# Edge pass: eight graphs a turn instead of four, the expert layer in two halves

## What is computed

```python
h = (x_flat @ W_gat).reshape(M, HEADS, NUM_EXPERTS)            # 4 heads, 4 experts
e = leaky_relu(a_src[src] + a_dst[dst])                         # one row per edge and head
ee = exp(e - segment_max(e, dst)[dst]); denom = segment_sum(ee, dst)
agg = segment_sum(h[src] * ee / denom[dst], dst) + b_gat
scores = layernorm(agg, gamma, beta).mean over the heads        # then top 2 of 4, softmax
for ei in range(4):
    out += g[ei] * (gelu(x @ W1[ei] + b1[ei]) @ W2[ei] + b2[ei])
```

## Time and profile before

| | us |
|---|---|
| median of 3 runs | 3323.31 (3321.15 to 3329.72) |
| profiled execution, span | 3908.9 |
| of it up to the first gather of edge rows | 1927.15 |
| busy over the span: PE, DVE, ACT, POOL | 1964.9, 2118.6, 1188.0, 1852.3 |

### The profile page before, as it was taken

One profiled execution on the slowest core, in us unless ns is written; L12 is line 12 of the kernel. 1 busy time (PEld: TensorE's weight loads), 2 busy tenths in 40 slices (PEclk: granted clock), 3 DMA queues, 4 the chain that ended last, 5 costly groups with the idle time before them and its releaser, 6 DMA issues. The chain is left out here.

```text
span 3908.9 us, 31732 instructions
## 1 busy us (share of the span) xinstructions
PE 1964.9 (50%) x9058; PEld 1350.2 (35%) x9113; DVE 2118.6 (54%) x4420; ACT 1188.0 (30%) x2437; POOL 1852.3 (47%) x1785
## 2 busy tenths in 40 slices
PE   0777742377777426676232445345244433444446
PEld 0666641255454215666211122122122212222223
DVE  7799887997789984444312334333233323433336
ACT  0676753244344204554201212112121111221212
POOL 5000247354444214445675555654655665556552
PEclk9988855699898657776556666666666666766668
DMA  6970001011111021001111111111111111111111
GB/s 212 345 292 1 17 26 34 22 35 47 34 44 30 31 84 38 17 21 22 41 28 32 28 31 37 26 34 27 32 30 31 37 26 34 27 38 33 28 31 38
DMA packets 172773, 197.65 MB, mean 51 GB/s; under 512 B 60217, under 2 KB 127072, under 8 KB 172032
## 3 DMA queue, kind: packets, MB, share of 16 engines
q1 hardware_dynamic: 107184, 118.69, 9.1%
q0 software_dynamic: 60160, 67.73, 8.4%
q10 hardware_dynamic: 5328, 9.97, 0.7%
HBM read 96.94 MB, written 105.25 MB: 52 GB/s over the span
## 5 line engine op out<-in xcount | busy, mean ns | idle before, releaser
L1453 POOL DMA_INDIRECT edge_rows<-node_table,edge_ids x1024 | 990.2, 967 | 687.3 <-POOLq L1193 385.9
L1581 PE MATMUL x_b_hid<-x_featT,x_w 128*128 128x512 f32 x512 | 353.6, 837 | 599.8 <-PEq L1193 395.7
L1096 POOL DMA_INDIRECT token_results<-arena,token_of x160 | 247.2, 1545 | 370.3 <-ACT arena L1030 271.4
L1581 PEld LDWEIGHTS x_b_hid<-x_featT,x_w 128*128 128x128 f32 x512 | 113.1, 254 | 830.7 <-issue 635.6
L1109 POOL DMA_INDIRECT adjacent<-keys,row_ids x256 | 243.0, 949 | 315.5 <-DVE counts L785 168.1
L1588 PE MATMUL x_b_res<-x_w,x_hid 128*128 128x128 f32 x2048 | 311.2, 304 | 146.1 <-issue 146.1
L1089 POOL DMA_INDIRECT slots<-arena,send x128 | 169.7, 1325 | 433.5 <-ACT arena L987 398.7
L1588 PEld LDWEIGHTS x_b_res<-x_w,x_hid 128*128 128x128 f32 x2048 | 275.9, 212 | 245.6 <-issue 245.4
L1415 DVE SCALAR_TENSOR_TENSOR x_weighed<-x_b_res,gates,x 128x128 f32<-128x128 f32 x128 | 36.1, 344 | 523.5 <-DVEq L1193 493.0
L562 DVE TENSOR_TENSOR sort_ping<-sort_pong 128x1024 f32<-128x1024 f32 (+1 forms) x184 | 285.8, 1594 | 47.5 <-ACT sort_pong L973 43.5
L562 DVE TENSOR_TENSOR sort_pong<-sort_ping 128x1024 f32<-128x1024 f32 (+1 forms) x184 | 285.7, 1594 | 37.0 <-ACT sort_ping L973 33.3
(11 more groups left out here) (333 smaller groups left out, 4303.3 us busy)
## 6 DMA issues: line engine op xcount, KB each, us to landing
edge_table<-zeros SPq DMA_DIRECT2D x8, 5120.0 KB
edge_rows<-node_table,edge_ids POOLq DMA_INDIRECT x1024
arena<-slots SPq DMA_DIRECT2D x40, 260.0 KB
slots<-zeros SPq DMA_DIRECT2D x2, 5120.0 KB
edge_table<-edge_rows SPq DMA_DIRECT2D x64, 160.0 KB
out_dram<-x_y ACTq DMA_DIRECT2D x33, 256.0 KB
adjacent<-in_adj_dram SPq DMA_DIRECT2D x32, 256.0 KB, 2.8
arena<-token_results SPq DMA_DIRECT2D x32, 256.0 KB
```

The lines of the kernel that those rows point to most:

```text
L1096: pool.indirect_dma_start(rows_dram, bass.IndirectOffsetOnAxis(token_of[:, n % 4, r:r + 1], 0), res[:, n % 2, r, :], None, bounds_check=TO ...
L1453: pool.indirect_dma_start(rows[:, u, c, :], None, table_dram, bass.IndirectOffsetOnAxis(ids[:, u, c:c + 1], 0)).then_inc(rows_in[u], 16)
L1581: pe.matmul(b_hid[:, c % 2, :], w1[:, c // HC1, c % HC1 * P:(c % HC1 + 1) * P], featT[:, :], start=True, stop=True).then_inc(hid_mm, 1)
```

## The change

A unit becomes eight graphs and a part 32 gathers, so there are 16 units, 16 turns and 32 parts. DVE and ACT treat the windows, the attention and the gates of eight graphs at once. The expert layer keeps tiles for four graphs (PER), and each of its engines handles a unit in two halves: ACT and PE one half after the other, each with its normalised x, transposes, hidden and output products; DVE, once all gates of the unit are made, waits for the first half's products, sums them, gives res_free, waits for the second half's, and sums them. One store of 512 KB a turn replaces two of 256. In PE the last expert's bias product moves behind its output products, and PE itself gives hid_free before it; DVE gave it before. The early scratch tiles wide, self_w and clamp_w move into win_msg.

```diff
-PART_TILES = 16
+PART_TILES = 32
-UNIT = 4
+UNIT = 8
+HALVES = UNIT // PER
@@ edges_and_experts1
-    SPAN = UNIT * NODES
+    SPAN = PER * NODES
-        self_w, clamp_w, wide = sb("self_w", [P, GRAPHS, HEADS]), sb("clamp_w", [P, GRAPHS, HEADS]), sb("wide", [P, GRAPHS, GAT])
+        early = msg[:, :, :, :].rearrange("p t k c -> p (t k c)")
+        wide = early[:, 0:GRAPHS * GAT].rearrange("p (n c) -> p n c", c=GAT)
...
-        feat, featT = sb("x1_feat", [P, UNIT, FEAT]), sb("x1_featT", [P, SPAN])
-        hid, weighed, y = sb("x1_hid", [P, E * HC1, SPAN]), sb("x1_weighed", [P, UNIT, FEAT]), sb("x1_y", [P, UNIT, FEAT])
+        feat, featT = sb("x1_feat", [P, PER, FEAT]), sb("x1_featT", [P, SPAN])
+        hid, weighed, y = sb("x1_hid", [P, E * HC1, SPAN]), sb("x1_weighed", [P, PER, FEAT]), sb("x1_y", [P, UNIT, FEAT])
@@ DVE
-                take(dve, res_mm, 1)
-                dve.sem_inc(hid_free, 1)
-
-                settle()
-                for e in range(E):
-                    if e == E - 1:
-                        take(dve, out_done, 16)
-                    for v in range(UNIT):
...
+                for h in range(HALVES):
+                    take(dve, res_mm, 1)
                     settle()
-                dve.sem_inc(summed, 1)
-                dve.sem_inc(res_free, 1)
+                    for e in range(E):
+                        if e == E - 1 and h == 0:
+                            take(dve, out_done, 16)
+                        for v in range(PER):
+                            at = h * PER + v
...
+                            last = dve.scalar_tensor_tensor(to, b_res[:, e, v, :], one[:, at, e:e + 1], so_far, ALU.mult, ALU.add)
+                            step(last)
+                        settle()
+                    dve.sem_inc(summed, 1)
+                    dve.sem_inc(res_free, 1)
@@ ACT
             def send(unit):
-                take(act, summed, 1)
+                take(act, summed, HALVES)
...
+                for h in range(HALVES):
+                    for v in range(PER):
+                        b = mine * UNIT + (h * PER + v)
...
+                    take(act, hid_free, 1)
+                    for c in range(E * HC1):
+                        act.wait_ge(hid_mm, c + 1)
+                        act.activation(hid[:, c, :], b_hid[:, c % 2, :], ACT.Gelu, bias=b1[:, c:c + 1]).then_inc(hid_s, 1)
+                    act.sem_inc(hid_mm, -E * HC1)
                 send(before)
@@ PE
-                    pe.matmul(b_res[:, e, :, :], ones[0:1, :], b2[0:1, e, :].unsqueeze(1).to_broadcast([1, UNIT, FEAT]), start=True, stop=False)
-                    for v in range(UNIT):
+                    final = e == E - 1
+                    if not final:
+                        pe.matmul(b_res[:, e, :, :], ones[0:1, :], b2[0:1, e, :].unsqueeze(1).to_broadcast([1, PER, FEAT]), start=True, stop=False)
+                    for v in range(PER):
...
-                last.then_inc(res_mm, 1)
+                last.then_inc(hid_free, 1)
+                pe.matmul(b_res[:, E - 1, :, :], ones[0:1, :], b2[0:1, E - 1, :].unsqueeze(1).to_broadcast([1, PER, FEAT]),
+                          start=False, stop=True).then_inc(res_mm, 1)
+
+            def turn():
+                for _ in range(HALVES):
+                    half()
```

More of the change, by code:

```diff
@@ L1147, in edges_and_experts1 @@
         msg, got, sums, adv = sb("win_msg", [P, UNIT, WINDOW, GAT]), sb("win_got", [P, UNIT, GAT]), sb("win_sums", [P, UNIT, HEADS]), sb("win_adv", [P, UNIT])
+        early = msg[:, :, :, :].rearrange("p t k c -> p (t k c)")
+        wide = early[:, 0:GRAPHS * GAT].rearrange("p (n c) -> p n c", c=GAT)
+        self_w, clamp_w = (early[:, lo:lo + GRAPHS * HEADS].rearrange("p (n h) -> p n h", h=HEADS)
+                           for lo in (GRAPHS * GAT, GRAPHS * (GAT + HEADS)))
         gat_b, gamma, beta = sb("gat_b", [P, GAT]), sb("gat_gamma", [P, GAT]), sb("gat_beta", [P, GAT])
@@ L1208, in _ @@
             dve.memset(left[:, GRAPHS:GRAPHS + UNIT], 0.0).then_inc(prepared, 1)
-            dve.memset(y[:, :, :], 0.0).then_inc(summed, 1)
+            dve.memset(y[:, :, :], 0.0).then_inc(summed, HALVES)
             made[0] += 1
@@ L1403, in turn @@
                 step(dve.tensor_tensor(one[:, :, :], one[:, :, :], per4(first[:, :]), ALU.mult))
-                take(dve, res_mm, 1)
-                dve.sem_inc(hid_free, 1)
-                settle()
-                for e in range(E):
-                    if e == E - 1:
-                        take(dve, out_done, 16)
-                    for v in range(UNIT):
[L1413 to L1416, removed]
-                    settle()
-                dve.sem_inc(summed, 1)
-                dve.sem_inc(res_free, 1)
+                for h in range(HALVES):
+                    take(dve, res_mm, 1)
+                    settle()
+                    for e in range(E):
[3 more added lines that the diff above has]
+                            at = h * PER + v
+                            so_far = x[:, bass.ds(unit * UNIT + at, 1), :].rearrange("p o f -> p (o f)") if e == 0 else weighed[:, v, :]
+                            to = y[:, at, :] if e == E - 1 else weighed[:, v, :]
+                            last = dve.scalar_tensor_tensor(to, b_res[:, e, v, :], one[:, at, e:e + 1], so_far, ALU.mult, ALU.add)
[3 more added lines that the diff above has]
+                    dve.sem_inc(res_free, 1)
                 take(dve, step_s, done[0])
@@ L1520, in send @@
             def send(unit):
-                take(act, summed, 1)
+                take(act, summed, HALVES)
                 act.dma_start(out[:, bass.ds(unit * UNIT, UNIT), :], y[:, :, :]).then_inc(out_done, 16)
             def turn(mine, before):
-                for v in range(UNIT):
[L1526 to L1536, removed]
+                for h in range(HALVES):
+                    for v in range(PER):
+                        b = mine * UNIT + (h * PER + v)
+                        last = act.activation(feat[:, v, :], x[:, bass.ds(b, 1), :].rearrange("p o f -> p (o f)"), ACT.Identity,
+                                              bias=shift[:, bass.ds(b, 1)], scale=rstd[:, bass.ds(b, 1)])
+                    last.then_inc(normed, 1)
+                    take(act, turned, 1)
+                    act.activation(featT[:, :], b_featT[:, :, :].rearrange("p v i -> p (v i)"), ACT.Copy).then_inc(featT_s, 1)
+                    take(act, hid_free, 1)
[3 more added lines that the diff above has]
+                    act.sem_inc(hid_mm, -E * HC1)
                 send(before)
@@ L1570, in _, with half @@
             pe.wait_ge(weights_in, 64)
-            def turn():
+            def half():
                 take(pe, normed, 1)
-                for v in range(UNIT):
+                for v in range(PER):
                     last = pe.transpose(b_featT[:, v, :], feat[:, v, :], ident)
@@ L1584, in turn @@
                 for e in range(E):
-                    pe.matmul(b_res[:, e, :, :], ones[0:1, :], b2[0:1, e, :].unsqueeze(1).to_broadcast([1, UNIT, FEAT]), start=True, stop=False)
-                    for v in range(UNIT):
+                    final = e == E - 1
+                    if not final:
+                        pe.matmul(b_res[:, e, :, :], ones[0:1, :], b2[0:1, e, :].unsqueeze(1).to_broadcast([1, PER, FEAT]), start=True, stop=False)
+                    for v in range(PER):
                         for c in range(HC1):
-                            last = pe.matmul(b_res[:, e, v, :], hid[:, e * HC1 + c, v * P:(v + 1) * P], w2[:, e * HC1 + c, :], start=False,
-                                             stop=(v == UNIT - 1 and c == HC1 - 1))
-                last.then_inc(res_mm, 1)
+                            last = pe.matmul(b_res[:, e, v, :], hid[:, e * HC1 + c, v * P:(v + 1) * P], w2[:, e * HC1 + c, :],
+                                             start=final and v == 0 and c == 0, stop=not final and v == PER - 1 and c == HC1 - 1)
+                last.then_inc(hid_free, 1)
[4 more added lines that the diff above has]
+                    half()
             pe.wait_ge(planned, 1)
```

2 lines of the change are left out of this document (1 added, 1 removed).

## The result

The changed kernel takes 3421.06 us (median of 4, 3414.72 to 3422.92) against 3322.82 us for the kernel before in the same runs: ratio 1.0296, 95% interval 1.0284 to 1.0309. That is 98 us slower, in the forecast's direction and inside the range of 3344 to 3440, though 1 us above the 3370 to 3420 that the forecast case itself allowed. The forecast was +70.

What follows compares the result with a forecast made beforehand. POOL's issue was taken to bound the loop. The end's 144.3 us, less 64.1 before and 10.1 for earlier last-but-one windows, gave +70.1 on 3323.3: 3394 us, range 3344 to 3440.

Steps and rivals of the forecast that it cites:

- the forecast case: Whole pass: 3394 us, 70.1 us slower, allowed from 3370 to 3420; chance 0.65.
- What bounds the loop: In the loop of the kernel before, POOL's issue sets the turn without stalls: 45.6 us against 29.
- The cover: In the changed loop, POOL's turn of 91.2 us hides the wait between the halves, whose chain has a 76.6 us cycle.
- Rival A: In the loop, the halves' chain overtakes POOL: 96 us a cycle, 3466 us in all; chance 0.15.
- The end: From the last-but-one windows' issue to the span's end, PE's pieces stand uncovered in series: 144.3 us, 64.1 before.
- a sign: In the changed kernel's trace, the last message product comes some 33 us after the last turn's first operation.
- The loop's 25 us: From first to last-but-one windows, the loop was forecast to change by -91.2 us; measured -66.6.
- the small gain on DVE's share of POOL's lengthened issues: In the loop, DVE's lengthening of POOL's issues was taken to change by nothing, between -10 and +10 us in all.

Runs made afterwards that it cites:

- the undisturbed trace: The kernel before, run again with no edit for a trace without the first one's stalls: 3322.99 us, trace span 3321.2 us.
- the changed kernel with the short product: The changed kernel with a message product of one graph instead of eight, the other seven graphs' messages left out: 3379.4 us, ratio 1.0193.

## Why the prediction was right, and where its size was off

**What bounds the loop.** Right. Taking 492 us of waits out of the trace, because the median had no room for them, gave a turn of 45.6, an end of 64.1 and a first stage of 1806 us; the undisturbed trace has 45.83, 64.0 and 1797.7.

**The cover.** Right. The wait between the halves, 15.0 to 20.9 us of DVE's time a turn, didn't move the turn when it was taken away (93.61 against 93.45). Rival A, the chain through two halves overtaking POOL, didn't come about: DVE waits 34.5 to 40.5 us for its windows in the turns after the first (40.10 in the line at 3284.47).

**The end.** The steps stood, with sizes off in both directions. From a turn's start to its gates it took 29.0 us (29.1 forecast), from the message product to the gates 19.8 (19.9). The last message product stands 88.9 us after the last-but-one turn's start (85.8): two terms of that stretch were mis-sized against each other. The output products of the second half took 20.85 us of waiting instead of 12.7, because I had priced them from a stretch in which PE had been at work just before. Here PE had been idle for 48 us, and the granted clock of the two stretches on either side of the sums is:

```profile
3318.00:3339.00 21.00, 20.31 (x74) 14.51 (x75) 0.23 (x1) 0.00 (x0) 0.00 (x0) 0.57 0.00 0
3339.00:3361.00 22.00, 20.25 (x94) 11.45 (x93) 10.91 (x29) 8.91 (x14) 0.00 (x0) 1.00 0.00 0
3337.70 1.12 PE L1599 MATMUL x_b_res<-x_b,ones 1*128 1x512 f32 x2
3348.85 1.09 PE L1593 MATMUL x_b_res<-x_b,ones 1*128 1x512 f32 x2 [0.87 <-PEq L1198]
3359.71 1.12 PE L1599 MATMUL x_b_res<-x_b,ones 1*128 1x512 f32 x2
```

In the first PE was granted 0.57 of full speed in the mean, near the lower of its two levels (1.2 GHz of 2.4), in the second 1.00, and the same output and bias products take 3337.70 + 1.12 - 3318.69 = 20.1 us there and 3359.71 + 1.12 - 3348.85 = 12.0 here. The pieces behind, at full clock, were shorter than mine: 10.1 instead of 12.4 us from the transposes to the first output product. The wait between the last halves was 15.46 us instead of 12.7, and the store after the last sum 3.2 instead of 4. The sum missed by 4.8 us. The trace's 20.85 us is the longest value of a wait that takes 15.0 us in other turns, so most of the 4.8 us can be chance. By the longer wait and the shorter pieces the last message product begins 28.4 us after the last turn's first operation, where the prediction named 33 as a sign.

**The loop's 25 us.** This is the step that failed: "the small gain on DVE's share of POOL's lengthened issues (45.6 against 36 x 1.25 = 45.0) I take at nothing, between -10 and +10 us in all, since as many elements pass." The lengthening doesn't go by elements. A gather that begins while the product runs waits for its end, so a product of 1.76 us costs 0.4 us in most turns and 1.2 in some, and one of 3.36 us costs 2.34 in every turn: 14 x 2.34 = 33 us against 30 x 0.54 = 16. The gather that is hit begins 0.89 or 0.90 us after the product's start in all 14 turns. That fits the order of the two engines, since the landing of POOL's windows starts DVE's turn. The trace that I predicted from had such a gather beside the product of its middle turn, and I averaged it away:

```profile
2728.20 1.36 POOL L1453 DMA_INDIRECT edge_rows<-node_table,edge_ids  x1 [0.30 <-issue]
```

The bound should have been from nothing to the product's full length, 15 x 3.4 = 50 us; the 25 us lie outside the 10 that I allowed. The number stayed in the range only because the range went half way to rival A, which didn't come about.

The Trainium skill, page "SBUF — State Buffer", section "Who interferes with whom", says that a DVE instruction with two SBUF inputs contends with a GpSimd instruction that reads SBUF, because its second input comes through the shared read interface, and that a tensor_reduce never contends on this chip. The trace agrees with both: the products (two inputs) lengthen gathers, and the gathers that begin in the 5.27 us reductions of the changed kernel stay at 0.94 to 0.95 us. The same section adds that in an earlier probe a tensor_tensor did not stall the DMA. For these indirect DMAs the measurement decides otherwise (2.34 us a turn, gone with the product). That it is the read of the indices that waits would fit both, but no run here separates it.

Of the Trainium skill's two rules on grouping (page "Perfetto Trace Analysis", section "Optimizing Scalar/DVE Operations") the second held. Grouping made DVE's work less, 565 us busy instead of 689, and the kernel slower; four message products for one made it more, 700 us against 688 in the undisturbed trace of the kernel before, and that kernel 17 us faster. The 689 of 1982 us that I named for it show only that DVE isn't saturated; the runs with the product in pieces are what bears the rule out.

## What to carry to other kernels

When one engine bounds a pipeline, work out the turn of that engine first, then the ends: doubling the step doubles what stands before the first result and after the last, and saves only on engines that had time. A resource that an instruction holds for its whole length costs by the length of the single instruction, not by the total; where the holder is off the critical path, cut it into pieces, since their overhead is free there. And when a trace is far longer than the median, build the sum without its waits and check it against the median before trusting either.

## What the runs showed of the hardware

An indirect DMA issue of 0.94 us on POOL that begins within a DVE product of two SBUF operands ends 0.8 us after the product's end (3.28 us long beside a product of 3.36); every gather or window issue above 1.0 us in the ten traces ends 0.81 to 0.84 us after such an instruction. Four such products back to back let it through after the one in which it began (1.42 us long). Issues that begin in a reduction of 5.27 us stay at 0.94 to 0.95. The same output products took 20.1 us when PE had idled for 48 us before them, 14.7 after 28 us, and 12.0 right behind other work; after 41 us of idling, in the changed kernel with the short product, they took 14.4, and with ACT's exponentials between the halves, in the last turn, 20.1 after 10 us, so the idle time alone doesn't settle it. The profiled execution of one program spanned 3908.9 us once and 3321.2 us another time, with medians of 3323 and 3318 us beside it.
